# Delta rule with one key product for two matrices, and the write keys shifted through DRAM

## The chip, the cores and the metric

The kernel runs on one core of one Trainium2 chip. All data are 32-bit floats. The metric is the device time of one execution in microseconds (us). A core has TensorE (PE, matrix products and turns of a block against an identity matrix), VectorE (DVE), ScalarE (ACT), GpSimd (POOL) and SyncE (SP), which in this program does nothing but issue DMAs. The five run their own instruction streams, in order, and wait for one another by semaphores.

## The reference, cut to what matters

The program is two layers of a recurrent network: a layer norm, a delta rule, a mixture of experts, a layer norm, a selective scan, a ternary feed-forward net. The change touches the delta rule alone, which has 4 sequences of 1024 rows, 2 heads of 128. `rk` are the read keys (rows of x, each scaled to length 1); the write keys `wk` are the same rows one row later. The reference works in chunks of 64 rows, the kernel in chunks of 128, which gives the same numbers.

```python
rk = rk / jnp.maximum(jnp.linalg.norm(rk, axis=-1, keepdims=True), 1e-12)
wk = jnp.pad(rk[:, :, :-1], ((0, 0), (0, 0), (1, 0), (0, 0)))
...
cum = jnp.cumsum(log_decay, -1)
L_mask = jnp.tril(jnp.exp(jnp.tril(cum[..., :, None] - cum[..., None, :])))
M = jnp.tril(-(wk_scaled @ jnp.swapaxes(wk, -1, -2)) * L_mask, -1)
A = solve_triangular(eye - M, jnp.broadcast_to(eye, M.shape), lower=True, unit_diagonal=True)
intra = jnp.tril(rk @ jnp.swapaxes(wk, -1, -2) * L_mask, -1)
...
def step(S, inp):
    A_i, vsc_i, wkd_i, rkd_i, intra_i, wkp_i, ced_i = inp
    v_new = A_i @ vsc_i - A_i @ wkd_i @ S
    o_i = rkd_i @ S + intra_i @ v_new
    S = ced_i[..., None, None] * S + wkp_i @ v_new
    return (S, o_i)
```

M needs the products of write keys with write keys, scaled by beta (a sigmoid per row) and a decay; intra needs those of read keys with write keys. Since wk is rk one row later, row t of the first matrix is row t-1 of the second up to the factors: the products are the same numbers, shifted by one.

## The kernel before

The time axis is cut into 8 chunks of 128 rows; one step n handles chunk n of all 4 sequences and both heads, so that most instructions are issued twice (h = 0, 1) on tiles of 128 partitions by 4 blocks of 128 (128x512). There are no loops over a scheduler's list: the code of each engine is written out by hand, in functions `sp_a`, `pool_a`, `dve_a`, `act_a` and `pe_a`. The lists `ahead` and `order` (L198, L199) name the steps that fill a PSUM bank in PE's order; from them the program gives out the 4 banks of each head in turn (`gbank`, `gfree`), and the lists of `g_dve`, `g_act` and `g_pool` number what each engine signals. A prime behind a name means chunk n+1, two primes n+2.

I call a turn of the loop `for n in range(NSEQ)` pass n. In pass n PE does: the product `kk` of write keys with write keys of chunk n+1; a turn `d4`; a turn `wkT` of the write keys of chunk n; `wkS`, write keys times state S; the levels 4, 5 and 6 that widen the inverse A from blocks of 16 to 128 rows (P4, D4, P5, t5, D5, t6, P6, T6, with the turn of the next read keys `rkT` before level 6); `MT`, a turn of M of chunk n+1; `vn`; the values `v` of chunk n+1; per head the output `o` and the state product `S`; the product `kq` of read keys with write keys of chunk n+1; and the output projection `y`, whose left operand is OT, ACT's copy of `o`. The keys lie turned in RKT: `prev(n, h)` are columns 0 to 127 (write keys) and `mine(n, h)` columns 1 to 128 (read keys) of 129.

The running sums `cum` of the log decays of a chunk are laid as a row in DRAM (cumd) and loaded into all 128 partitions, as tile ZR (`sums`, L310). From ZR ACT makes three masks: E for M (relu L886, exp L891; with log beta, as bias `nbc`, per partition), ET for intra (relu L900, exp L911, cut to a triangle by POOL as ETsel), and ez (L908) for the read keys times decay, rkdT, which POOL makes. ZR is one tile per head, so the next sums are issued only after ETr and ez of the former.

DVE multiplies bank `kk` by E into M (`mix`, L545) and bank `kq` by ET into iT (`inner`, L561). SP stores the 16x16 blocks of M on the diagonal to DRAM (`blocks`, L317, tile md) and loads them into MB (`spread`, L325), each spread over 16 partitions; POOL inverts them by 31 small steps (`solve`, tiles X and Y); DVE puts X on the diagonal of DT (`inverse`, L551), with which PE begins the levels. In pass n SP issues, in this order: the blocks, the spread, the sums of chunk n+2, the results of pass n-1 (`sd<-XS`), and rows for the expert stage, which POOL scatters by 64 indirect DMAs between its solves (from pass 2 on).

ACT's code for a pass is the following; OT is the last copy before `squares`.

```python
                copy("d4", n, "d4", "Dm")
                if more:
                    copy("wk", n, "wkT", "wk")
...
                if more:
                    upper(n + 1)
                    decays(n + 1, "ET")
...
                copy("vn", n, "vn", "vn")
...
                if n + 2 < NSEQ:
                    lower(n + 2)
                for h in range(2):
                    e.wait_ge(*g_pe[h].at("o", n))
...
                    e.activation(OT[h][:], four(gbank("o", n, h)), ACT.Copy).then_inc(g_act[h].sem, 1)
```

## Time and profile before

| | |
|---|---|
| median of 3 runs | 2403.66 us (2401.52 to 2408.75) |
| the profiled execution's own time | 2399.99 us |
| its span | 2398.3 us |
| busy, share of the span | PE 92%, DVE 77%, ACT 69%, POOL 60% |
| chain that ended last | PE 54%, DVE 13%, issue 9%, ACT 9%, DMA 6%, POOL 6% |
| passes 0 to 7 of the delta rule | about 88 to 404 us of the span |
| mean DMA rate | 179 GB/s |

The span is the part of the execution that the profiler covers; the profiled execution's own time is 1.7 us more. "Busy" is the time in which an engine ran an instruction, summed over all stages of the program, so the shares of the table say little on the delta rule; the views by stretch do. In a timeline, each row is a run of like instructions: its start in the span, how long it lasted, the engine, the line of the kernel, what it writes and reads, how many there were, and in brackets how long the engine had stood idle before it and for what.

### The profile page before, as it was taken

The page shows a single profiled execution, that of the slowest core. Times are in us where ns is not written, and L with a number is a line of the kernel's source. Part 1 is how long each engine was busy: PE and PEld are TensorE (multiplying, and loading weights), DVE is VectorE, ACT ScalarE, POOL GpSimd, SP SyncE. Part 2 cuts the span into 40 slices and gives each one's busy share as a digit, 9 for nine tenths or more (in the row PEclk, how much of TensorE's full clock was granted, in tenths as well). Part 3 has the DMA queues.
Part 4 walks back from the last instruction along what each step waited for, and adds up shares of the span by engine and source line. Part 5 has one row for each costly group of instructions (what it writes and reads, how often), then busy time and mean ns, then how long its engine had stood idle before and what let it go on. Part 6 is the DMA issues. An engine that isn't in the chain of part 4 may idle for free.

```text
span 2398.3 us, 36952 instructions
## 1 busy us (share of the span) xinstructions
PE 2197.5 (92%) x12464; PEld 1788.7 (75%) x12464; DVE 1843.5 (77%) x2832; ACT 1646.8 (69%) x2715; POOL 1449.4 (60%) x1026
## 2 busy tenths in 40 slices
PE   6799897999999999996999999999999999999986
PEld 4788796998898898884667667676676765776765
DVE  5574453667766666677989989989899899898995
ACT  6775542555555556666887788787877877888774
POOL 0236563111111113336988989889889898898895
PEclk8899998999999999997999999999999999999988
DMA  8434544566666654444655655555555555565563
GB/s 291 85 56 111 112 125 136 181 236 232 234 230 230 233 209 152 133 126 154 219 169 190 198 184 186 194 186 202 176 186 195 199 187 177 185 211 177 178 208 101
DMA packets 235434, 430.22 MB, mean 179 GB/s; under 512 B 35089, under 2 KB 117457, under 8 KB 235234
## 3 DMA queue, kind: packets, MB, share of 16 engines
q1 hardware_dynamic: 229090, 410.87, 53.0%
q0 software_dynamic: 6144, 16.79, 2.2%
q8 instruction: 113, 1.85, 0.3%
q14 instruction: 87, 0.71, 0.1%
HBM read 353.61 MB, written 73.96 MB: 178 GB/s over the span
## 4 chain that ended last, share of the span: by engine, by line
PE 54%; DVE 13%; issue 9%; ACT 9%; DMA 6%; POOL 6%; SPq 1%; another core or an unknown queue 1%; POOLq 1%; DVEq 0%; ACTq 0%
PE pb L1641 11%; PE pb L1614 11%; DVE pb L2094 6%; PE pb L2406 5%; PE pb L2411 5%; PE pb L994 3%; PE pb L2305 2%; PE pb L2432 2%; PE pb L2321 2%; DVE UU L2100 2%; DMA XB<-xnd 2%; PE pb L2330 2%; DMA CC<-bcd 2%; POOL UU L2019 2%; POOL UU L2027 1%
## 5 line engine op out<-in xcount | busy, mean ns | idle before, releaser
L2019 POOL TENSOR_TENSOR UU<-dx,BB 128x1024 f32<-128x1024 f32 x256 | 614.6, 2409 | 112.0 <-DMA BB<-bcd 83.6
L2231 ACT ACTIVATE pb<-dt,al 128x512 f32<-128x512 f32 x512 | 339.5, 685 | 149.4 <-DVE UU L2100 147.8
L2100 DVE TENSOR_TENSOR UU<-pb,CC 128x512 f32<-128x512 f32 x512 | 351.3, 686 | 24.3 <-DMA CC<-bcd 6.5
L2094 DVE TENSOR_TENSOR_SCAN pb<-pb,hs,UU 128x512 f32<-128x512 f32 x256 | 328.5, 1283 | 10.7 <-ACT pb L2231 7.4
L2094 DVE TENSOR_TENSOR_SCAN pb<-pb,UU 128x512 f32<-128x512 f32 x256 | 313.0, 1223 | 8.5 <-ACT pb L2231 7.9
L1381 POOL TENSOR_TENSOR clo_b<-craw_b,chi_b 128x1024 fp32r<-128x1024 f32 x22 | 62.3, 2830 | 405.9 <-ACT chi_b L1444 405.9
L1531 DVE TENSOR_TENSOR HL<-HF,HH 128x512 fp32r<-128x512 f32 x220 | 159.6, 728 | 179.9 <-ACT HH L1436 165.7
L2406 PE MATMUL pb<-HAh,WH 128*128 128x512 f32 x1024 | 282.7, 419 | 7.0 <-DVE dt L2075 5.1
L1431 ACT ACTIVATE HF<-pb,BU 128x512 f32<-128x512 f32 x192 | 132.3, 689 | 219.4 <-PE pb L1614 191.9
L2411 PE MATMUL pb<-HAl,WH 128*128 128x512 f32 x1024 | 259.7, 396 | 0.0
L1641 PE MATMUL pb<-W2h,HH 128*128 128x256 f32 x880 | 256.0, 291 | 1.0
L1641 PE MATMUL pb<-W2l,HH 128*128 128x256 f32 x880 | 248.6, 282 | 0.0
L1641 PE MATMUL pb<-W2h,HL 128*128 128x256 f32 x880 | 248.5, 282 | 0.0
L2406 PEld LDWEIGHTS pb<-HAh,WH 128*128 128x128 f32 x1024 | 191.5, 193 | 67.2 <-issue 27.5
L2027 POOL TENSOR_TENSOR UU<-UU,UU 128x1024 f32<-128x1024 f32 x96 | 230.8, 2404 | 5.6 <-DVE UU L2100 5.6
L2411 PEld LDWEIGHTS pb<-HAl,WH 128*128 128x128 f32 x1024 | 195.4, 191 | 44.4
L2305 PEld LDWEIGHTS pb<-ident,UU 128*128 128x128 f32 x1280 | 147.7, 143 | 58.6 <-POOL UU L2027 38.5
L2305 PE MATMUL pb<-ident,UU 128*128 128x128 f32 x1280 | 165.5, 277 | 20.7 <-POOL UU L2027 19.9
L1641 PEld LDWEIGHTS pb<-W2h,HH 128*128 128x128 f32 x880 | 167.5, 190 | 12.0 <-DVE HL L1531 4.8
L1641 PEld LDWEIGHTS pb<-W2h,HL 128*128 128x128 f32 x880 | 167.8, 191 | 5.9 <-issue 1.0
L1641 PEld LDWEIGHTS pb<-W2l,HH 128*128 128x128 f32 x880 | 167.6, 190 | 0.0
L2045 POOL TENSOR_TENSOR HAl<-tg,HAh 128x512 fp32r<-128x512 f32 x128 | 162.9, 1297 | 5.4 <-ACT HAh L2269 5.4
(336 smaller groups left out, 4891.0 us busy)
## 6 DMA issues: line engine op xcount, KB each, us to landing
WH<-fhd SPq DMA_DIRECT2D x176, 512.0 KB, 3.5
BB<-bcd SPq DMA_DIRECT2D x256, 256.0 KB, 4.7
CC<-bcd SPq DMA_DIRECT2D x256, 256.0 KB, 5.0
raw<-in_w1a SPq DMA_DIRECT2D x23, 1024.0 KB, 7.3
raw<-in_w2a SPq DMA_DIRECT2D x23, 1024.0 KB, 7.4
craw_b<-in_fch SPq DMA_DIRECT2D x22, 512.0 KB, 5.9
fhd<-chi_b SPq DMA_DIRECT2D x22, 512.0 KB, 3.9
fld<-clo_b SPq DMA_DIRECT2D x22, 512.0 KB, 4.9
```

Source lines behind the costliest of these rows:

```text
L1531: e.tensor_tensor(HH[q % 4][1][:], HF[q % 2][:], HH[q % 4][0][:].bitcast(F32), ALU.subtract).then_inc(s_hl, 1)
L1614: t = e.matmul(bk[:, a * wide:(a + 1) * wide], wt_[:, k, c_], xt_[k], start=(n == 0), stop=(n == 5))
L1641: t = e.matmul(to[:, j * D:(j + 1) * D], ht[:, c_], wt_[:, row, :], start=(row == 0 and j == 0 and m == 0), stop=(row == 7 and m == 2), sk ...
L2019: e.tensor_tensor(ubuf(n)[:], dx[p][:], BB[n % 3][:].rearrange("p (a m) -> p a m", a=1).to_broadcast([P, 2, 512]), ALU.mult).then_inc(p_u. ...
L2027: e.tensor_tensor(ubuf(n)[:], ubuf(n)[:], ubuf(n - 1)[:], ALU.add).then_inc(p_join.sem, 1)
L2045: e.tensor_tensor(hl[:, it, :], ttile("h", blk, j)[:], hh[:, it, :].bitcast(F32), ALU.subtract).then_inc(f_pool.sem, 1)
L2094: e.tensor_tensor_scan(h_[:], h_[:], uu[:, c, :], first, ALU.mult, ALU.add).then_inc(v_sc.sem, 1)
L2100: e.tensor_tensor(uu[:, c, :], abank(n, c)[:], CC[n % 3][:], ALU.mult).then_inc(v_mu.sem, 1)
L2231: e.activation(abank(n, c)[:], dt[p][:, c, :], ACT.Exp, scale=al1[:, 2 * p + c, s:s + 1]).then_inc(c_a.sem, 1)
L2305: t = e.matmul(ypart(j, c), ubuf(n)[:, c, j * P:(j + 1) * P], ident[:], is_transpose=True, start=False, stop=(s == 15), skip_group_check=True)
L2406: e.matmul(bk[:], WH[n % 3][:, c_], xh_, start=(k == 0), stop=False)
L2411: t = e.matmul(bk[:], WH[n % 3][:, c_], xl_, start=False, stop=(k == 7))
```

## The change

**One product.** `kk` and the turn `MT` stay for chunk 0 alone. For every later chunk the bank of `kq` gives both matrices: its columns 0 to 126 times E make columns 1 to 127 of the turned M, and all of it times ET makes iT. So M is made turned from the start (tiles MTB, two in rotation, in place of M2 and the copies MT), and iT has two tiles (iTB). For this E needs, along the row, cum less log beta, and per partition cum: cumd and ZR become twice as wide (128x4x256 for each head, 512 KB instead of 256 KB as loaded), and the prologue makes the second row by one more product and a tile `nl`. `kq` of chunk n+1 moves from the end of pass n to its start, where `kk` was, and DVE's `inner(n + 1)` from behind S to behind `mix(n + 1)`.

**The write keys.** PE's turn `wkT` and ACT's copies to `wk` go. In their place ACT's `rk` rows are stored to DRAM (`keys_out`, tile rkd, 256 KB for each head) and loaded one row higher (`keys_in`) as `wk`.

**The masks.** ET of chunk n+2 is made in pass n, behind E, in place of ET of chunk n+1 in the middle of pass n. POOL's cut of ET stands behind the solve instead of ahead of it.

```diff
+            def keys_out(n):
+
+                for h in range(2):
+                    e.wait_ge(*g_act[h].at("rk", n))
+                    e.dma_start(rkd[h, :, 1 + n * P:1 + (n + 1) * P, :].rearrange("b t d -> t b d"), TB[h]["rk"][:]).then_inc(s_rkd, 16)
+
+            def keys_in(n):
+
+                e.wait_ge(s_rkd, 32 + 32 * (n + 1))
+                for h in range(2):
+                    if n:
+                        e.wait_ge(*g_pe[h].at("S", n - 1))
+                    e.dma_start(TB[h]["wk"][:], rkd[h, :, n * P:(n + 1) * P, :].rearrange("b t d -> t b d")).then_inc(s_wk, 16)
...
                 if n + 1 < NSEQ:
                     spread(n + 1)
+                if 0 < n < NSEQ - 1:
+                    keys_in(n)
                 if n + 2 < NSEQ:
+                    keys_out(n + 2)
                     sums(n + 2)
...
                     scatter(chunk_pairs(n - 1)[2:])
-                    upper(n + 1)
                     decayed(n + 1)
                     solve(e, n + 1)
+                    if n + 2 < NSEQ:
+                        upper(n + 2)
...
-                e.tensor_tensor(M2[:, h], four(gbank("kk", n, h)), W["E"][:], ALU.mult).then_inc(g_dve[h].sem, 1)
...
+                e.tensor_tensor(MTB[n % 2][:, h, :, 1:P], four(gbank("kq", n, h))[:, :, 0:P - 1], W["E"][:, :, 1:P], ALU.mult).then_inc(g_dve[h].sem, 1)
...
                 if more:
                     for h in range(2):
                         mix(n + 1, h)
+                    for h in range(2):
+                        inner(n + 1, h)
...
                 if more:
                     for h in range(2):
-                        inner(n + 1, h)
-                    for h in range(2):
                         inverse(n + 1, h)
...
                 copy("d4", n, "d4", "Dm")
-                if more:
-                    copy("wk", n, "wkT", "wk")
                 if n + 2 < NSEQ:
                     rows_(n + 2)
-                if more:
-                    upper(n + 1)
-                    decays(n + 1, "ET")
...
                 copy("t6", n, "t6", "DT")
-                if more:
-                    copy("MT", n + 1, "MT", "MT")
                 copy("vn", n, "vn", "vn")
...
                 if n + 2 < NSEQ:
                     lower(n + 2)
+                    upper(n + 2)
+                    decays(n + 2, "ET")
...
                 if more:
-                    for h in range(2):
-                        e.wait_ge(*g_act[h].at("rc", n))
-                        kk(n + 1, h)
+                    inner(n + 1)
                 for h in range(2):
                     e.wait_ge(*g_dve[h].at("DT", n))
                     turned("d4", n, h, TB[h]["DT"])
-                for h in range(2 if more else 0):
-                    turned("wkT", n, h, prev(n, h))
...
-                if more:
-                    for h in range(2):
-                        MT(n + 1, h)
...
-                if more:
-                    inner(n + 1)
                 for b2 in range(2):
                     y(n, b2)
```

What this does to the order of instructions is plainest in three places. A number behind a name tells tiles of the same role apart (E_95 is head 0, E_108 head 1; the change gives the tiles other numbers).

ACT at the end of pass 0, before:

```order
L916 ACTIVATE MT_97<-pb 128x512
L916 ACTIVATE MT_110<-pb 128x512
L916 ACTIVATE vn_102<-pb 128x512
L916 ACTIVATE vn_115<-pb 128x512
L886 ACTIVATE E_95<-ZR_164,sm_nbc 128x128 x4
L886 ACTIVATE E_108<-ZR_165,sm_nbc 128x128 x4
L891 ACTIVATE E_95<-E_95 128x512
L891 ACTIVATE E_108<-E_108 128x512
L974 ACTIVATE OT_125<-pb 128x512
L974 ACTIVATE OT_126<-pb 128x512
```

and with the change:

```order
L952 ACTIVATE vn_101<-pb 128x512
L952 ACTIVATE vn_112<-pb 128x512
L920 ACTIVATE E_96<-ZR_164,sm_cum 128x128 x4
L920 ACTIVATE E_107<-ZR_165,sm_cum 128x128 x4
L927 ACTIVATE E_96<-E_96 128x512
L927 ACTIVATE E_107<-E_107 128x512
L936 ACTIVATE ET_97<-ZR_164,sm_cum 128x128 x4
L936 ACTIVATE ET_108<-ZR_165,sm_cum 128x128 x4
L947 ACTIVATE ET_97<-ET_97 128x512
L947 ACTIVATE ET_108<-ET_108 128x512
L1009 ACTIVATE OT_125<-pb 128x512
L1009 ACTIVATE OT_126<-pb 128x512
```

The copies MT are gone, and the ten instructions of ET stand between E and OT.

SP in pass 1, before:

```order
L317 DMA md<-M_121 128x1x16 x8
L325 DMA MB<-md 16x1920 x8
L310 DMA ZR_164<-cumd 128x4x128
L310 DMA ZR_165<-cumd 128x4x128
L331 DMA sd<-XS 128x256 x4
```

and with the change:

```order
L321 DMA md<-MTB_118 128x1x16 x8
L329 DMA MB<-md 16x1920 x8
L344 DMA wk_94<-rkd 128x4x128
L344 DMA wk_105<-rkd 128x4x128
L336 DMA rkd<-rk_92 128x4x128
L336 DMA rkd<-rk_103 128x4x128
L314 DMA ZR_164<-cumd 128x4x256
L314 DMA ZR_165<-cumd 128x4x256
L349 DMA sd<-XS 128x256 x4
```

Four DMAs of the keys stand ahead of the sums, which are twice as wide.

PE at the start of pass 1 (behind y of pass 0), before:

```order
L994 MATMUL pb<-RKT 128x128 x8
L986 MATMUL pb<-ident,DT_99 128x128 x4
L986 MATMUL pb<-ident,DT_112 128x128 x4
L986 MATMUL pb<-ident,RKT 128x128 x8
L994 MATMUL pb<-S,RKT 128x128 x8
L994 MATMUL pb<-Dm_98,MT_97 128x128 x4
```

and with the change:

```order
L1029 MATMUL pb<-RKT 128x128 x8
L1021 MATMUL pb<-ident,DT_99 128x128 x4
L1021 MATMUL pb<-ident,DT_110 128x128 x4
L1029 MATMUL pb<-S,RKT 128x128 x8
L1029 MATMUL pb<-Dm_98,MTB_118 128x128 x4
```

The first row was kk and is now kq; the turn of the write keys has gone from between d4 and wkS.

## Rows read from the trace of the kernel before

**Rows 1.** Stretches: us; busy PE, PEld, DVE, ACT, POOL; PE clock; DMA share; GB/s.
```profile
122.40:159.90 37.50, 35.80 (x309) 34.31 (x309) 26.92 (x77) 26.39 (x70) 13.93 (x35) 1.00 0.34 57
...
240.90:281.40 40.50, 35.95 (x305) 33.67 (x304) 20.80 (x46) 24.13 (x68) 24.18 (x46) 1.00 0.56 105
```

**Rows 2.** Timelines of ACT and PE, ends of passes 1 and 4.
```profile
148.98 2.45 ACT L886 ACTIVATE E<-ZR,sm_nbc 128x128 f32<-128x128 f32 x8 [2.45 <-DMA ZR<-cumd]
...
156.45 3.62 PE L1033 MATMUL pb<-wr,OT 128*128 128x256 f32 x16
...
273.30 2.44 ACT L886 ACTIVATE E<-ZR,sm_nbc 128x128 f32<-128x128 f32 x8 [7.32 <-DMA ZR<-cumd]
...
277.89 3.69 PE L1033 MATMUL pb<-wr,OT 128*128 128x256 f32 x16 [1.82 <-ACT OT L974]
```

**Rows 3.** View of the tile ZR, 100 to 330 us: idle before it, landing.
```profile
  DMA ZR<-cumd: 28.7, 6
...
DMA to landing us min/median/max: 7.7/9.9/14.3
```

**Rows 4.** Timeline of SP in pass 1 (the time is that of issuing).
```profile
126.61 5.05 SPq L317 DMA_DIRECT2D md<-M  x8
132.93 3.58 SPq L325 DMA_DIRECT2D MB<-md  x8
136.60 0.93 SPq L310 DMA_DIRECT2D ZR<-cumd  x2
```

**Rows 5.** Timeline of PE in pass 1: products and turns, with what follows.
```profile
122.43 1.95 PE L994 MATMUL pb<-RKT 128*128 128x128 f32 x16
124.22 1.04 PE L986 MATMUL pb<-ident,DT 128*128 128x128 f32 x8
125.09 1.04 PE L986 MATMUL pb<-ident,RKT 128*128 128x128 f32 x8
...
143.02 1.09 PE L986 MATMUL pb<-ident,M 128*128 128x128 f32 x8
143.95 1.95 PE L994 MATMUL pb<-vsc,DT 128*128 128x128 f32 x16
...
151.09 1.06 PE L994 MATMUL pb<-vnt,wk 128*128 128x128 f32 x8
```

**Rows 6.** Timeline of ACT, middle of pass 1.
```profile
129.12 2.44 ACT L900 ACTIVATE ET<-ZR,sm_cum 128x128 f32<-128x128 f32 x8
131.58 1.28 ACT L911 ACT_TABLE_LOAD   x1
132.87 1.15 ACT L911 ACTIVATE ET<-ET 128x512 f32<-128x512 f32 x2
```

**Rows 7.** Timeline of DVE, passes 1 and 6.
```profile
155.91 1.44 DVE L561 TENSOR_TENSOR iT<-pb,ET 128x512 f32<-128x512 f32 x2
...
361.66 1.29 DVE L551 TENSOR_TENSOR DT<-X,mask 128x512 f32<-128x512 f32 x2 [0.89 <-POOL X L388]
```

**Rows 8.** POOL behind MB's landing, pass 1; DMA view 221:226 and 24:36; tile TM.
```profile
142.36 0.29 POOL L381 COPY X<-eye 128x128 f32<-128x128 f32 x1 [3.54 <-DMA MB<-md]
...
DMA packets 451, 0.23 MB, mean 46 GB/s; under 512 B 5, under 2 KB 451, under 8 KB 451
...
q1 hardware_dynamic: 451, 0.23, 24.8%
...
DMA packets 3596, 4.73 MB, mean 394 GB/s; under 512 B 143, under 2 KB 3211, under 8 KB 3595
...
DMA to landing us min/median/max: 5.1/5.1/5.1
```

**Rows 9.** Busy time by stretch around a wait of pass 3.
```profile
205.90:210.20 4.30, 0.01 (x1) 0.00 (x0) 0.79 (x3) 4.28 (x15) 1.92 (x2) 0.93 0.38 101
210.30:216.30 6.00, 6.00 (x28) 6.00 (x29) 3.41 (x8) 2.05 (x3) 1.23 (x2) 0.50 0.99 145
```

**Rows 10.** Timeline of DVE in pass 5, behind the scatter.
```profile
294.50 1.12 DVE L717 SCALAR_TENSOR_TENSOR vsc<-pb,sm_bec,vsc 128x128 f32<-128x128 f32 x4 [8.98 <-remote]
```

More of the change, by code:

```diff
@@ L109, in program @@
         sm = {k: sbt("sm_" + k, [P, NT, 2]) for k in ("beta", "nbeta", "g", "cum", "nbc", "ec", "bec", "tl", "tail", "ced")}
+        sm["nl"] = sbt("sm_nl", [P, NT, 2])
         sm.update({k: sbt("sm_" + k, [P, NT, 4]) for k in ("ab", "l")})
         S = sbt("S", [P, 2, B, P])
-        nm = ["rk", "ez", "wk", "vsc", "E", "ET", "MT", "Dm", "DT", "Pm", "iT", "vn", "vnt"]
+        nm = ["rk", "ez", "wk", "vsc", "E", "ET", "Dm", "DT", "Pm", "vn", "vnt"]
         TB = [{k: sbt(f"{k}{h}", [P, 4, P]) for k in nm} for h in range(2)]
         RD = [[sbt(f"rkdT{h}{i}", [P, 4, P]) for i in range(2)] for h in range(2)]
-        M2 = sbt("M2", [P, 2, 4, P])
+        MTB = [sbt(f"MTB{i}", [P, 2, 4, P]) for i in range(2)]
+        iTB = [sbt(f"iTB{i}", [P, 2, 4, P]) for i in range(2)]
         MB = sbt("MB", [P, 15, 8, 16])
@@ L147, in program @@
         rows = [sbt(f"rows{i}", [P, 2, D]) for i in range(3)]
-        cumT = sbt("cumT", [64, P])
-        ZR = [sbt(f"ZR{h}", [P, 4, P]) for h in range(2)]
+        cumT = sbt("cumT", [64, 2, P])
+        ZR = [sbt(f"ZR{h}", [P, 4, 2, P]) for h in range(2)]
         a_end = at[0]
@@ L331, in residuals @@
                     e.dma_start(sd[:, n + 8 * b, :], XS[:, n + 8 * b, :]).then_inc(s_sd, 16)
+            e.dma_start(rkd[:, :, 0, :].rearrange("h b d -> (h b) d"), zt[0:8, 0:P]).then_inc(s_rkd, 16)
+            keys_out(0)
             e.wait_ge(*a_dve.at("cumT"))
-            e.dma_start(cumd, cumT[:]).then_inc(s_zr, 16)
+            e.dma_start(cumd, cumT[:].rearrange("p k t -> p (k t)")).then_inc(s_zr, 16)
             e.wait_ge(s_zr, 16)
@@ L384, in solve @@
                 if k % 2:
-                    e.tensor_tensor(Y16[:, :, r:15], MB[:, r:15, :, r].rearrange("p r g -> p g r"),
+                    col = MB[:, r, :, r + 1:16] if n else MB[:, r:15, :, r].rearrange("p r g -> p g r")
+                    e.tensor_tensor(Y16[:, :, r:15], col,
                                     X16[:, :, r:r + 1].to_broadcast([P, 8, 15 - r]), ALU.mult).then_inc(g_x.sem, 1)
@@ L539, in mix @@
                 W = TB[h]
-                e.wait_ge(*g_pe[h].at("kk", n))
                 e.wait_ge(*g_act[h].at("E", n))
-                if n:
-                    e.wait_ge(*g_pe[h].at("MT", n - 1))
-                    e.wait_ge(s_md, 128 * n)
-                e.tensor_tensor(M2[:, h], four(gbank("kk", n, h)), W["E"][:], ALU.mult).then_inc(g_dve[h].sem, 1)
+                if n == 0:
+                    e.wait_ge(*g_pe[h].at("kk", 0))
+                    e.tensor_tensor(MTB[1][:, h], four(gbank("kk", 0, h)), W["E"][:], ALU.mult).then_inc(g_dve[h].sem, 1)
+                    return
+                e.wait_ge(*g_pe[h].at("kq", n))
+                e.wait_ge(*(g_pe[h].at("MT", 0) if n == 1 else g_pe[h].at("P6", n - 2)))
+                e.wait_ge(s_md, 128 * (n if n == 1 else n - 1))
+                e.tensor_tensor(MTB[n % 2][:, h, :, 1:P], four(gbank("kq", n, h))[:, :, 0:P - 1], W["E"][:, :, 1:P], ALU.mult).then_inc(g_dve[h].sem, 1)
             def inverse(n, h):
@@ L885, in lower @@
                     for b in range(4):
-                        t = e.activation(W["E"][:, b, :], z_[:, b, :], ACT.Relu, bias=sm["nbc"][:, n + 8 * b, h:h + 1])
+                        if n:
+                            t = e.activation(W["E"][:, b, :], ZR[h][:, b, 1, :], ACT.Relu, bias=sm["cum"][:, n + 8 * b, h:h + 1], scale=-1.0)
+                        else:
+                            t = e.activation(W["E"][:, b, :], z_[:, b, :], ACT.Relu, bias=sm["nbc"][:, n + 8 * b, h:h + 1])
                     t.then_inc(g_act[h].sem, 1)
@@ L907, in decays @@
                             e.wait_ge(*g_pool[h].at("rkdT", n - 1))
-                        e.activation(TB[h]["ez"][:], ZR[h][:] if n else four(gbank("z", 0, h)), ACT.Exp).then_inc(g_act[h].sem, 1)
+                        e.activation(TB[h]["ez"][:], ZR[h][:, :, 0, :] if n else four(gbank("z", 0, h)), ACT.Exp).then_inc(g_act[h].sem, 1)
                     else:
@@ L934, in act_a @@
             rows_(1)
-            copy("MT", 0, "MT", "MT")
+            for h in range(2):
+                e.wait_ge(*g_pe[h].at("MT", 0))
+                e.activation(MTB[0][:, h], four(gbank("MT", 0, h)), ACT.Copy).then_inc(g_act[h].sem, 1)
             carried(0)
@@ L1121, in pe_a @@
                         if l == 4:
-                            e.wait_ge(*g_act[h].at("MT", n))
+                            if n:
+                                e.wait_ge(*g_dve[h].at("M", n))
+                            else:
+                                e.wait_ge(*g_act[h].at("MT", 0))
                             e.wait_ge(*g_act[h].at("d4", n))
```

59 lines of the change are left out of this document (35 added, 24 removed).

## The prediction

> **What bounds the kernel now.** I read the busy time by stretch first, then the timelines of PE, ACT and SP inside one pass, then the view of the tile ZR, then the DMA view. The change touches only the delta rule, from about 55 to 404 us of 2398. A pass is one turn of the loop over n; it runs from one kk product to the next (122.4 to 159.9 us is pass 1, 240.9 to 281.4 us pass 4) [rows 1].
>
> The reader is to see two things. First, PE is nearly full: 35.8 us busy in the 37.5 us of pass 1 [rows 1]. That speaks for the change. Second, ACT is not full, but it works to a deadline at the end of each pass. It sits idle until the running sums ZR have landed (2.45 us in pass 1, 7.32 us in pass 4), then makes E, then copies OT, and PE's y product waits for OT [rows 2]. In pass 4 PE already stands 1.82 us for it. All six passes that load sums show this idle time, 28.7 us in all [rows 3]. The sums are issued at 136.60, as the last thing behind md (5.05 us of issue) and MB (3.58 us), and are ready at 148.98: 12.4 us later [rows 2, 4]. So there are two chains of about equal length: PE's own work, and M, md, MB, ZR, E, OT, y. The change shortens the first and lengthens the second.
>
> **The change, part by part.** *Products.* In each pass with a successor PE loses one product of both heads (1.95 us as a row, 1.79 from its start to that of the turn behind it), the turn of wk (1.04; the turn ahead of it takes 0.87 from its start to the next) and the turn of M (1.09, 0.93 up to the next) [rows 5]: 3.6 us, 25 us in seven passes. ACT loses the copies of both, about 1.1 us each. This counts only where PE is last. Worked for pass 1, in us after its start at 122.4: PE would be ready for y at 156.45 - 3.6 - 122.4 = 30.4.
>
> *ET moves.* The relus and exps of ET, 2.44 and 1.15 us [rows 6], leave the middle of the pass, where ACT had time, and stand between E and OT. From E's start to y it takes 4.6 us today when nothing else holds y (273.30 to 277.89) [rows 2]; with ET it takes 4.6 + 3.6 = 8.2. Pass 1 had 7.5 us from E to y (148.98 to 156.45), so it loses 0.7; pass 4 loses 3.6; the other four idled 18.9 us together before E, 4.7 each, between the two, and get 2.0 each. Sum 12. Ahead of the first pass ET also stands before the copy of d4: 3 of its 3.6 us count.
>
> *Sums are issued later.* SP now issues the load of wk and the store of rk ahead of the sums. A pair like it takes 0.93 us [rows 4], so 1.9 us, in pass 0 (store alone) 0.9. The order of SP's queue is the changed program's own. Where the sums wait for the exp ez rather than for SP, two other things stand there: the table load, 1.28 us, which lay ahead of ET's exp [rows 6] and now lies ahead of ez, behind t5; and the two iT products of DVE, 1.44 us [rows 7], which come ahead of Pm instead of after S. Pm feeds D4, D5 and t5, and ez stands behind t5; no row says how much of it DVE's gaps take up, so I take 1.1, between 0 and 1.44. Of 1.9 on the one path and 1.28 + 1.1 = 2.4 on the other I take 2.1 us for each of the six passes: 13. The page "ScalarE: Activation LUTs" of the Trainium skill, section "What ACT_TABLE_LOAD costs", adds a drain of about 1.38 us to each load. Here the exp starts 1.29 us after the load starts [rows 6]; the trace disagrees, and by that rule the sum would be 4 us more over three passes.
>
> *Sums land later.* The store and the load of keys are 1 MB in 2048 pieces of 512 bytes per pass, ahead of the sums; the sums themselves double to 1 MB. No row has these transfers. Bounds for the keys: 0, if they fill gaps; 23 us, if they go as the queue does while sums are under way (451 packets in 5 us, 46 GB/s) [rows 8]. The nearest row is the loading and zeroing at the start, 3596 packets in 12 us, so 6.8 us for 2048 [rows 8]; I take it, because those too read and write distinct addresses. Bounds for the doubling: 0, since the number of pieces stays, or 6.6 us (pass 1: MB landed 142.36, sums ready 148.98) [rows 2, 8]; I take 2.5. In pass 1 the sums are then ready at 142.4 + 6.8 + 6.6 + 2.5 = 158.3 against 148.98 + 1.9 = 150.9: 7.4 more. The same in pass 4; 5 in pass 0, with the store alone; 2 each in passes 2, 3 and 5, where sums are issued some microseconds behind MB and keys drain meanwhile. Sum 26.
>
> *PE's clock.* PE would be ready for y about 31.5 us into a pass and get OT at 37 or later: 6 us or more idle. After 4.3 us idle the granted clock was 0.50, the 1.2 GHz level, through the next 6 us [rows 9], against 1.00 in pass 4, which holds the 1.82 us wait [rows 1]. Half speed for 6 us costs at most 3; part of it lies beside DVE. 2.7 for six passes: 16; bounds 0 and 18.
>
> *At nothing.* wk by DMA: in pass 1 its load would stand first behind MB (landed 142.36) and, at the keys' rate taken above (6.8 us for both), be there after 3.4 us more plus some 2 for landing: 147.8, against its product S at 151.09 less the 1.8 us of the two turns [rows 5, 8]. A margin of 1.5 us is thin; without it S, and with it o and OT, would come later by what is missing, but OT now waits longer for ET anyway. Pass 6 has no E or ET, but its end waits for the solve on POOL (DT, 0.89 us of idle time behind X) [rows 7], so PE's 3.6 us are worth nothing there. The scatter's first eight transfers now wait for ET; they run beside the idle PE. One more product in the prologue, the extra row of cumd and the first rk store: below 1 us.
>
> **Sum.** 12 + 3 + 13 + 26 + 16 = 70. The profiled execution took 2399.99 us; 2400 + 70 = 2470. That execution lies 3.7 us under the median of the runs shown, well inside my range. No change, for this kernel, means within 0.3%, 7 us.
>
> **Rivals.** *A, the sums come early (faster).* If they land as an ordinary load does, ZR's 12.4 us shrink. TM, 512 KB, landed in 5.1 us [rows 8]; two such would be ready about 6.5 us after issue. Pass 1 would last 14.2 (to the issue of the sums) + 2.1 + 6.5 + 8.2 + 3.6 = 34.6 instead of 37.5 us; with half of that where the scatter runs some 10 us are gained: 2390. It decides once the sums are ready less than about 9 us after issue (14.2 + 2.1 + 9 + 8.2 + 3.6 = 37.1). For it: pieces grow from 512 to 1024 bytes. Against it: 7.7 to 14.3 us to landing today [rows 3], and 2048 pieces more ahead of them. [...] *B, within 0.3%:* the sums at 9 to 10 us after issue and no drop of the clock, so that what ET costs and what PE gives back cancel. *C, the sums go by bytes:* 12.4 us become 25; six times 12.4 instead of six times 2.5 is 59 more, 2530. For it: one row is read by 128 partitions, and the rate stayed near 46 GB/s with the DMA engines a quarter busy [rows 8]. *D, the scatter collides:* twelve indirect transfers in a row across the start of a pass, as in pass 5, where DVE stood 8.98 us [rows 10]. It would add about 5 us in three passes: 2485. *E, PE remains the bound:* all 25 us come, 2375; it needs OT at 30.4 us, that is sums ready 6 us after issue; part of A's chance.
>
> **Numbers.** Forecast 0.70, A with E 0.07, B 0.05, C 0.10, D 0.08. Faster 0.07, same 0.05, slower 0.88. Low end: ET, the start and the later issue alone, 12 + 3 + 13 = 28, less 3 if the later issue is partly hidden: 2425. High end: C with some of D, 2540. The likeliest is 2470.
>
> **What will show it.** In the new profile: the idle time of PE ahead of y, with ACT's OT as its releaser, in each of passes 0 to 5, 6 us or more; passes 1 and 2 at 45 to 52 us, pass 1 having had 37.5; ZR still above 10 us to landing; ACT's E, exp, ET, exp, OT in one run behind the landing; a granted clock of about a half ahead of and in y. PE's busy time outside slowed stretches is down 3.6 us a pass. The prediction is wrong if PE's idle time ahead of y is below 2 us, if the sums are ready within 9 us of issue, or if S waits for wk.

## The result, and the profile after

| | before | after |
|---|---|---|
| median of the device time, 5 runs each | 2403.66 us | 2453.61 us |
| lowest and highest | 2400.01, 2414.59 | 2447.82, 2456.65 |
| ratio, with its 95% interval | | 1.0200 (1.0178 to 1.0223) |
| the profiled execution's own time | 2399.99 us | 2456.65 us |
| its span | 2398.3 us | 2454.9 us |

The kernel became 2% slower, 50 us by the medians; 2470 was forecast, with 2425 to 2540 as the range. The two profiled executions lie 57 us apart.

The page of the changed kernel, the shares of busy time and the chain that ended last:

```profile
PE 2189.8 (89%) x12244; PEld 1779.6 (72%) x12244; DVE 1843.3 (75%) x2833; ACT 1631.2 (66%) x2687; POOL 1444.4 (59%) x1026
...
PE 53%; DVE 12%; ACT 10%; issue 10%; DMA 8%; POOL 5%; SPq 1%; POOLq 1%; another core or an unknown queue 0%; DVEq 0%; ACTq 0%
```

PE has less to do and its share fell from 92% to 89%. In the chain DMA went from 6% to 8%. Where the time lies is plain in the two timelines of ACT and PE at the end of pass 1, which answer to [rows 2]:

```profile
165.76 2.44 ACT L920 ACTIVATE E<-ZR,sm_cum 128x128 f32<-128x128 f32 x8 [8.17 <-DMA ZR<-cumd]
168.11 1.13 ACT L927 ACTIVATE E<-E 128x512 f32<-128x512 f32 x2
169.15 2.43 ACT L936 ACTIVATE ET<-ZR,sm_cum 128x128 f32<-128x128 f32 x8
171.48 1.13 ACT L947 ACTIVATE ET<-ET 128x512 f32<-128x512 f32 x2
172.52 1.05 ACT L1009 ACTIVATE OT<-pb 128x512 f32<-128x512 f32 x2
```

```profile
164.83 1.06 PE L1029 MATMUL pb<-vnt,wk 128*128 128x128 f32 x8
173.72 5.88 PE L1068 MATMUL pb<-wr,OT 128*128 128x256 f32 x16 [7.83 <-ACT OT L1009]
179.43 1.95 PE L1029 MATMUL pb<-RKT 128*128 128x128 f32 x16
```

The reader is to see one unbroken run on ACT behind the landing of the sums (E, exp, ET, exp, OT) and beside it PE, done at 165.9 and idle for 7.83 us. Then y takes 5.88 us, where it took 3.62. The busy time by stretch shows the whole of pass 1, the idle time, and y (columns as in [rows 1]):

```profile
134.50:179.40 44.90, 34.69 (x277) 32.43 (x276) 26.25 (x74) 23.13 (x64) 13.47 (x35) 0.89 0.45 83
...
165.90:173.70 7.80, 0.00 (x0) 0.01 (x1) 2.32 (x6) 7.80 (x24) 1.23 (x2) 0.63 0.05 16
173.70:179.50 5.80, 5.78 (x17) 4.75 (x18) 1.01 (x4) 4.47 (x18) 0.00 (x0) 0.62 0.00 0
```

SP in pass 1 answers to [rows 4]:

```profile
137.30 5.05 SPq L321 DMA_DIRECT2D md<-MTB  x8
143.62 4.35 SPq L329 DMA_DIRECT2D MB<-md  x8
148.07 0.93 SPq L344 DMA_DIRECT2D wk<-rkd  x2
149.04 1.06 SPq L336 DMA_DIRECT2D rkd<-rk  x2
150.20 3.87 SPq L314 DMA_DIRECT2D ZR<-cumd  x2
```

From issue to E's start it is now 15.6 us (150.20 to 165.76), against 12.4. In the code E waits for the sums of both heads, and SP needs 3.87 us to issue the two DMAs instead of 0.93: the second is issued at 153.3 us and lands 12.4 us later, just ahead of E. The view of the tile ZR, 90 to 400 us, gives the idle time of ACT ahead of E and the landing, answering to [rows 3]:

```profile
  DMA ZR<-cumd: 55.0, 6
...
DMA to landing us min/median/max: 7.9/12.5/14.0
```

**Where the 57 us lie.** A pass of 0 to 5 can be cut into four pieces that follow one another without a gap: from its start to the issue of the sums, from there to E, from E to y, and y. The pieces are read from the timelines of each profiled kernel; a pass starts where y of the pass before ends, the first piece of pass 0 counts from the span's start, and each sum is over passes 0 to 5, in us.

| kernel | to issue | issue to E | E to y | y | passes 6 and 7 | y of pass 7 ends |
|---|---|---|---|---|---|---|
| before | 194.2 | 77.3 | 33.4 | 21.9 | 77.6 | 404.4 |
| after | 204.3 | 90.8 | 47.8 | 35.5 | 80.6 | 458.9 |
| difference | 10.1 | 13.4 | 14.4 | 13.6 | 3.0 | 54.5 |

Another 2 us came about behind the delta rule. The column of passes 6 and 7 is made of pass 6, 40.7 us against 36.7, and pass 7, 39.9 against 40.9.

The piece from issue to E holds two things, the time in which SP issues the two DMAs and the landing of the second. SP's part is 16.1 us in the six passes, against 5.6 before; without it 74.6 us are left, against 71.7. So of the 13.4 us only 2.9 are later landing, and 10.5 are slower issuing.

### The profile page after: what moved, and what is told of

The parts are those of the page before. It is cut to its first block, busy times and chain, and to the rows that moved or that the text cites. A ratio compares the mean times of both kernels' runs of the same rounds, so it can differ in the third digit from the quotient of the medians.

```text
span 2454.9 us, 36493 instructions
## 1 busy us (share of the span) xinstructions
PE 2189.8 (89%) x12244; PEld 1779.6 (72%) x12244; DVE 1843.3 (75%) x2833; ACT 1631.2 (66%) x2687; POOL 1444.4 (59%) x1026
## 4 chain that ended last, share of the span: by engine, by line
PE 53%; DVE 12%; ACT 10%; issue 10%; DMA 8%; POOL 5%; SPq 1%; POOLq 1%; another core or an unknown queue 0%; DVEq 0%; ACTq 0%
PE pb L1672 11%; PE pb L1645 11%; DVE pb L2125 6%; PE pb L2437 5%; PE pb L2442 5%; DMA ZR<-cumd 4%; PE pb L2336 2%; PE pb L2352 2%; PE pb L1029 2%; PE pb L2463 2%; PE pb L2405 2%; PE pb L2361 2%; DMA XB<-xnd 2%; DVE UU L2131 2%; DMA CC<-bcd 2%
```

## The experiments

Every kernel below is the changed kernel with one edit, unless it says otherwise. The ratio is to the kernel before on the same chip. The chips differ: the kernel before took 2403.03 us beside the four kernels from et_behind_ot to warm, 2412.11 beside keys_around and the three from early_head to early_tail, 2401.30 beside scatter_first and early_scatter, and 2407.33 beside early_split and before_ez. So ratios are the safer comparison across these groups.

| kernel | median, us | ratio to before (95% interval) |
|---|---|---|
| the change | 2453.61 | 1.0200 (1.0178 to 1.0223) |
| et_behind_ot | 2448.55 | 1.0180 (1.0151 to 1.0210) |
| no_keys | 2428.00 | 1.0112 (1.0081 to 1.0144) |
| sums_single | 2445.85 | 1.0170 (1.0142 to 1.0199) |
| warm | 2448.79 | 1.0189 (1.0162 to 1.0216) |
| keys_around | 2429.69 | 1.0078 (1.0053 to 1.0104) |
| scatter_first | 2433.50 | 1.0136 (1.0119 to 1.0153) |
| early_head | 2428.81 | 1.0072 (1.0049 to 1.0096) |
| early_wk | 2424.96 | 1.0058 (1.0031 to 1.0085) |
| early_tail | 2417.46 | 1.0030 (1.0012 to 1.0047) |
| early_scatter | 2396.31 | 0.9985 (0.9968 to 1.0001) |
| early_split | 2393.21 | 0.9935 (0.9914 to 0.9956) |
| before_ez (edit of the kernel before) | 2409.18 | 1.0007 (0.9989 to 1.0024) |

And the pieces of those that change one thing, as in the table above:

| kernel | to issue | issue to E | E to y | y | passes 6 and 7 | y of pass 7 ends |
|---|---|---|---|---|---|---|
| et_behind_ot | 228.1 | 82.6 | 27.5 | 31.0 | 83.7 | 452.9 |
| no_keys | 192.5 | 75.7 | 47.8 | 35.2 | 80.7 | 431.9 |
| sums_single | 202.1 | 83.9 | 47.8 | 35.5 | 80.2 | 449.4 |
| warm | 206.1 | 89.2 | 53.5 | 27.6 | 77.5 | 454.0 |
| keys_around | 191.7 | 77.0 | 47.8 | 33.2 | 80.8 | 430.4 |
| scatter_first | 191.7 | 89.7 | 47.8 | 35.8 | 74.2 | 439.1 |

### The keys ahead of the sums: no_keys, keys_around

```diff
-                if 0 < n < NSEQ - 1:
-                    keys_in(n)
                 if n + 2 < NSEQ:
-                    keys_out(n + 2)
                     sums(n + 2)
```

(The waits for these DMAs go with them.)

> The changed kernel without the stores and loads of the keys in the passes: wk keeps the rows of chunk 0 for all chunks, so the state product is made from the wrong rows; times only. Theory as forecast: the 1 MB of keys ahead of the sums costs both issue time (1.9 us a pass) and landing time. From the issue of the sums to E it takes 15.1 us on the mean of six passes in the changed kernel and 12.9 in the kernel before; without keys it should be back near 13, and the issue comes 1 to 2 us earlier: 12 + 8 = 20 us less, 2434. Rival (the keys fill gaps, the landing is longer because the sums have doubled): issue to E stays at 15, and only the issue comes earlier, 2446.

Measured: 2428. Issue to E fell from 90.8 to 75.7 us, 12.6 a pass, so the rival falls: sums of twice the width land as fast as the single ones did in the kernel before (77.3) once no keys are ahead of them. Of the 15.1 us, 10.5 are SP's time for issuing the sums (16.1 us in six passes with the change, 5.6 here), and 4.5 are landing. The issue came 12 us earlier in all, more than the 8 expected.

keys_around keeps every byte and moves only the place in SP's queue:

```diff
+                if 0 < n < NSEQ - 1:
+                    keys_in(n)
                 if n + 1 < NSEQ:
                     blocks(n + 1)
...
-                if 0 < n < NSEQ - 1:
-                    keys_in(n)
                 if n + 2 < NSEQ:
-                    keys_out(n + 2)
                     sums(n + 2)
+                    keys_out(n + 2)
```

> The changed kernel with SP's order in a pass turned: the load of wk ahead of the blocks of M (SP waits there for M anyway), the sums right behind the spread, the store of rk behind the sums. All transfers stay. Without keys the kernel took 2428, with them 2454: 26 us. If it is the order (keys issued and queued ahead of the sums), most of that comes back: issue of the sums to E near 12.6 us, 2432. Rival (it is the bytes in the queue, wherever they stand; the store now runs beside the landing sums): issue to E stays at 15 and only the 1.9 us of issue come back, 2446.

Measured: 2429.69, ratio 1.0078, and issue to E 77.0 us. Its SP, ACT and PE in pass 1:

```profile
145.12 0.93 SPq L314 DMA_DIRECT2D ZR<-cumd  x2
146.10 3.58 SPq L336 DMA_DIRECT2D rkd<-rk  x2
149.73 3.85 SPq L349 DMA_DIRECT2D sd<-XS  x4
160.04 3.00 SPq L344 DMA_DIRECT2D wk<-rkd  x2
```

```profile
157.06 2.44 ACT L920 ACTIVATE E<-ZR,sm_cum 128x128 f32<-128x128 f32 x8 [2.72 <-DMA ZR<-cumd]
```

```profile
165.03 3.69 PE L1068 MATMUL pb<-wr,OT 128*128 128x256 f32 x16 [2.39 <-ACT OT L1009]
```

E starts 11.9 us behind the issue although the store of keys is issued right behind the sums; the load of the next wk stands at the end of the pass, where the queue is empty. Pass 1 takes 37.3 us, and 37.5 in the kernel before. SP issues the sums in 0.93 us in five of the six passes. So it was the order and not the bytes: of the 2.0% that the change costs, 1.2 points went with the places in SP's queue (0.9 with no_keys, whose interval overlaps this one). Whether the load or the store did more was not tried apart.

### The doubled sums: sums_single

```diff
-                    e.dma_start(ZR[h][:].rearrange("p b k t -> p b (k t)"), cumd.rearrange("(b n h) t -> n h b t", b=4, n=8)[n, h].rearrange("(o b) t -> o b t", o=1).to_broadcast([P, 4, 2 * P])).then_inc(s_zr, 16)
+                    e.dma_start(ZR[h][:, :, 0, :], cumd.rearrange("(b n h) t -> n h b t", b=4, n=8)[n, h, :, 0:P].rearrange("(o b) t -> o b t", o=1).to_broadcast([P, 4, P])).then_inc(s_zr, 16)
...
-                            t = e.activation(W["E"][:, b, :], ZR[h][:, b, 1, :], ACT.Relu, bias=sm["cum"][:, n + 8 * b, h:h + 1], scale=-1.0)
+                            t = e.activation(W["E"][:, b, :], ZR[h][:, b, 0, :], ACT.Relu, bias=sm["cum"][:, n + 8 * b, h:h + 1], scale=-1.0)
```

> The changed kernel with the sums loaded in single width (512 bytes a piece, 256 KB a head), E being made from the row that ET uses; the factor beta is left out of M, times only. If the doubling is worth 2.5 us a pass, as forecast, from the issue of the sums to E takes 12.6 instead of 15.1 us and the time falls by 15 us to 2439. If pieces count and bytes do not, both stay: 2454. If bytes set the landing (rival C) it would fall by 6 us or more a pass, 2418.

Measured: 2445.85. Issue to E is 83.9 us, 14.0 a pass: 1.2 less than with double width, between the first two answers. Of these 6.9 us in six passes 3.0 are again SP's issuing (13.2 us against 16.1). By the times alone the intervals of this kernel and of the change overlap (1.0142 to 1.0199, 1.0178 to 1.0223). With no_keys beside it, the doubling costs at most about 1 us a pass behind the keys, and nothing that shows without them. Rival C, landing by bytes, falls.

### ET behind OT: et_behind_ot

```diff
                     lower(n + 2)
-                    upper(n + 2)
-                    decays(n + 2, "ET")
                 for h in range(2):
                     e.wait_ge(*g_pe[h].at("o", n))
...
+                if n + 2 < NSEQ:
+                    upper(n + 2)
+                    decays(n + 2, "ET")
```

> The changed kernel with ET's relus and exps of chunk n+2 moved behind the copy to OT; nothing else. Theory (the chain ZR, E, ET, OT, y sets the length of passes 0 to 5): from E's start to y it takes 4.6 us instead of 7.96 in each of six passes, PE's idle time ahead of y falls from 7.8 to about 4.5 us in passes 1 to 3, and the time falls by about 20 us, to 2434. Rival (another wait ends at the same time as OT, so ET is covered): PE's idle time ahead of y keeps its length under another releaser, and the time stays at 2454. Second rival: ET now delays the copy of d4 at the start of the next pass and half is given back, 2444.

Measured: 2448.55. E to y fell to 4.59 us in every pass, 20.2 us in all, as the theory has it. But the piece up to the issue grew by 23.7 us. The second rival is right in kind, by another road than the copy of d4 alone, and more is given back than the half that it had (2448.55 against 2444). ACT and DVE at the start of pass 1:

```profile
123.09 2.44 ACT L936 ACTIVATE ET<-ZR,sm_cum 128x128 f32<-128x128 f32 x8
125.42 1.14 ACT L947 ACTIVATE ET<-ET 128x512 f32<-128x512 f32 x2
129.91 1.28 ACT L965 ACT_TABLE_LOAD   x1
131.21 0.21 ACT L965 ACTIVATE rn<-rn 128x8 f32<-128x8 f32 x1
131.32 1.06 ACT L952 ACTIVATE Dm<-pb 128x512 f32<-128x512 f32 x2
```

```profile
131.45 0.17 DVE L603 TENSOR_SCALAR rn<-rn 128x8 f32<-128x8 f32 x1 [6.64 <-ACT rn L965]
```

The squares and the square root of the key norms stand behind OT on ACT, and now behind ET too. The first instruction of a pass on DVE waits for that root, and M, the blocks and the sums stand behind it on DVE and SP. A deadline that the change had not touched lay 4 to 5 us behind OT.

### PE kept busy ahead of y: warm

```diff
                 e.wait_ge(*gfree("y", n, b2))
+                for j in range(36 if b2 == 0 and n < NSEQ - 2 else 0):
+                    e.matmul(bk[:, 0:P], ident[:], ident[:], start=True, stop=True)
```

> The changed kernel with 36 products of the identity matrix into y's own bank ahead of y in passes 0 to 5 (y overwrites them), so that PE is busy for about 8 us of the wait for OT. Theory (y is slow, 5.9 instead of 3.6 us, because PE stood idle ahead of it): y takes 3.6 us again in passes 1 to 3, less surely in passes 4 and 5, where 5 us of idle time are left; the time falls by 9 to 14 us, to 2440 to 2445. Rival (the granted clock follows something else, such as the load of the whole chip): y stays at 5.9 us and the time at 2454.

Measured: 2448.79, where 2440 to 2445 were expected. The busy time by stretch of this kernel, the wait and y of pass 1:

```profile
165.50:172.00 6.50, 6.50 (x61) 6.50 (x60) 0.94 (x2) 6.47 (x20) 1.22 (x2) 1.00 0.01 1
172.00:175.60 3.60, 3.60 (x20) 3.19 (x19) 0.00 (x0) 3.39 (x14) 0.00 (x0) 1.00 0.00 0
```

With PE busy through the wait the granted clock is 1.00 and y takes 3.62 us in passes 0 to 3; in passes 4 and 5, where 4.5 and 5.8 us of idle time are left, it takes 6.6 and 6.5. So the slow y comes from the idle time, and the rival falls. The products themselves held y up in passes 0 to 3 by 0.4 to 3.5 us (E to y 53.5 against 47.8), so of the 7.9 us won in y little is left, and by time this kernel is not told apart from the change.

### The scatter's place: scatter_first

The changed kernel cuts ET on POOL behind the solve and ahead of the scatter of two pairs of rows. This edit swaps the two:

```diff
                     solve(e, n + 1)
-                    if n + 2 < NSEQ:
-                        upper(n + 2)
                 else:
                     scatter(chunk_pairs(n - 1)[2:])
                 scatter(chunk_pairs(n)[:2])
+                if n + 2 < NSEQ:
+                    upper(n + 2)
```

> The changed kernel with the same move alone: POOL's scatter right behind the solve, the cut of ET behind it. In passes 3 to 5 the scatter's stalls lie beside the wait for OT, so little is to be had there; pass 6, 40.7 us against 36.7 before, has no such wait and should be back at 37, and ez and with it the sums come some us earlier in passes 3 to 5 (they stand behind t5 at 18 to 24 us into the pass). 4 us from pass 6 and up to 2 us in each of three passes: 2446. Rival (pass 6 is longer for another reason, such as iT ahead of the levels): 2454.

Measured: 2433.5, 20 us less than the change by the medians and 15 by the ratios, where 8 were expected. In the changed kernel the start of pass 6 (378.35 us) looked as follows on POOL (the fifth and the last of a row of twelve), DVE and PE:

```profile
378.23 0.96 POOL L475 DMA_INDIRECT xg<-rows,sl  x1 [0.31 <-issue]
...
387.10 0.96 POOL L475 DMA_INDIRECT xg<-rows,sl  x1 [0.30 <-issue]
```

```profile
390.40 1.13 DVE L749 SCALAR_TENSOR_TENSOR vsc<-pb,sm_bec,vsc 128x128 f32<-128x128 f32 x4 [6.93 <-remote]
```

```profile
385.79 1.53 PE L1029 MATMUL pb<-Dm,MTB 128*128 128x128 f32 x8 [3.00 <-issue]
391.00 2.04 PE L1029 MATMUL pb<-Dm,MTB 128*128 128x128 f32 x8 [3.68 <-issue]
```

POOL had waited 8.27 us for ET, so the eight indirect DMAs of the end of pass 5 began only at 373.06 us and ran on into the four of pass 6, and PE and DVE stood 6.7 and 6.9 us beside the end of the row and up to 3 us behind it, for nothing that the profile names. With the scatter ahead, the eight and the four are parted (the eighth starts at 362.29 us, the ninth at 367.79). Pass 6 of this kernel, and behind it that of the kernel before, are

```profile
364.90:398.10 33.20, 30.79 (x267) 29.29 (x266) 18.75 (x41) 7.09 (x14) 17.12 (x38) 1.00 0.69 171
```

```profile
326.60:363.30 36.70, 34.44 (x297) 32.80 (x296) 19.55 (x44) 12.50 (x28) 21.88 (x43) 1.00 0.60 155
```

It is 33.2 us long, 7.5 less than with the change and 3.5 less than before: here, in a pass without sums, PE's saving is seen in full. But the larger part of the gain is in the passes with sums. Passes 3 to 5 are 4.0, 5.2 and 1.8 us shorter, 11.0 together, where up to 6 were expected; their sums were issued 7.3, 1.5 and 2.2 us earlier. So the cost of the scatter's place was not hidden beside the wait for OT: with the sums later, OT came later too. (Another 2.6 us are in pass 0, where nothing is scattered yet; this edit does not explain them.)

### Taking the sums off the path: early_wk, early_tail, early_head

These three make ET and ez of chunk n+2 behind OT of pass n, so that ZR is free at the end of the pass, and move the squares and the root to the middle of the next pass, behind the rk rows (which takes away what undid et_behind_ot).

```diff
                 if n + 2 < NSEQ:
                     rows_(n + 2)
+                if n + 3 < NSEQ:
+                    for b in range(4):
+                        squares((n + 3 + 8 * b,))
+                    roots(n + 3)
...
                 if more:
-                    decays(n + 1, "ez")
                     carried(n + 1)
...
                     lower(n + 2)
-                    upper(n + 2)
-                    decays(n + 2, "ET")
...
+                if n + 2 < NSEQ:
+                    upper(n + 2)
+                    decays(n + 2, "ET")
+                    decays(n + 2, "ez")
```

early_wk takes the write keys as the kernel before does (turn and copy). early_tail keeps them in DRAM, in the order of keys_around. early_head is early_tail with `sums(n + 2)` as the first thing in SP's pass.

> The changed kernel with the write keys turned by PE and copied by ACT as in the kernel before (no keys through DRAM), ET and ez of chunk n+2 made behind OT in pass n, so that ZR is free at once and SP issues the next sums right behind the spread, about 14 us into each pass, and the squares and square roots in the middle of the pass. If the chain through ZR is what costs, E is made about 27 us into the pass, PE's idle time ahead of y is below 1 us, passes 1 and 2 take 36 us or less and the sum of the delta rule comes under the kernel before: 2392. Rival: passes 2 to 5 are held by the scatter on POOL and the stalls beside it, so they stay near 44 us and the time is 2410.

> As early_wk, but with the keys through DRAM in the order of keys_around. PE has 0.9 us and ACT 1.1 us less to do in a pass; the sums land later by what the keys cost there. If the order of SP has healed the keys, 2390; if their bytes still delay the sums by 2.5 us, E comes about 30 us into a pass and y waits 2 us: 2405.

> As early_tail, but the sums of chunk n+2 are issued as the first thing of pass n, ahead of the blocks of M. The chain through ZR is then some 14 us shorter and E never waits; passes 1 and 2 should be PE's own 34 us, 2378 in all. Rival: 1 MB of sums and 512 KB of keys now run beside md and MB, MB lands later than 20 us into the pass and DT waits for the solve: passes stay at 37 us or more, 2400.

Measured: 2424.96, 2417.46 and 2428.81. Pass 1 does what was expected of the first two (36.1 and 35.1 us), pass 2 does not quite (38.5 and 38.3 us, where 36 or less were expected of early_wk). In all three y waits for OT in none of passes 0 to 6, and y takes 3.69 us in passes 0 to 5. The keys through DRAM are worth 1 us in pass 1; by time early_wk and early_tail are not told apart. But passes 3 to 6 of early_tail take 45.7, 46.6, 45.6 and 54.5 us, and what stands there is again the scatter, on POOL at the end of pass 4 and on DVE in it:

```profile
291.88 1.22 POOL L455 TENSOR_SCALAR_AFFINE_SELECT ET<-ET 128x512 f32<-128x512 f32 x2 [14.29 <-ACT ET L947]
```

```profile
264.13 1.29 DVE L758 TENSOR_TENSOR Pm<-pb,mask 128x512 f32<-128x512 f32 x2 [11.07 <-remote]
```

ET comes later still, so twelve indirect DMAs run in a row across the start of each of passes 3 to 6 (246.64 to 261.6 us at the start of pass 4), and DVE stands 11.07 us. The misses of early_wk and early_tail have this cause, as early_scatter below confirms; the rival of early_wk named it, though with 2410 it too fell short. Pass 6 is not all loss: a second row of twelve runs within it, which in the other kernels falls into pass 7, and pass 7 takes 26.5 us instead of some 40. In early_head E never waited for ZR, as expected, but its own rival is right as well, in one pass: in pass 0, the blocks' way to MB is now shared with 1 MB of sums. POOL waits 20.57 us for MB (11.20 in early_tail), and DT for the solve; pass 1 takes 44.5 us, against 35.1 in early_tail:

```profile
118.68 0.29 POOL L407 COPY X<-eye 128x128 f32<-128x128 f32 x1 [20.57 <-DMA MB<-md]
```

```profile
130.74 2.13 DVE L584 TENSOR_TENSOR DT<-X,mask 128x512 f32<-128x512 f32 x2 [7.12 <-POOL X L415]
```

### Both together: early_scatter, early_split

early_scatter is early_tail with the swap of scatter_first. early_split also puts POOL's rkdT between the two groups of indirect DMAs:

```diff
+                    decayed(n + 1)
                     if chunk_pairs(n - 1):
                         e.wait_ge(*g_dve[1].at("M", n + 1))
                     scatter(chunk_pairs(n - 1)[2:])
-                    decayed(n + 1)
                     solve(e, n + 1)
```

> As early_tail, with POOL's scatter of two pairs of rows right behind its solve, as in the kernel before, and its cut of ET (upper) behind that. In early_tail POOL waits 14 us with the scatter behind it for ET, then issues 12 indirect DMAs in a row across the start of the pass, and DVE stands 11.07 us until they end; passes 3 to 5 take 46 us and pass 6 takes 54. Theory (the scatter's place is what is left): the stall falls to that of four DMAs in a row, passes 3 to 5 take 38 to 42 us and pass 6 below 42; the time falls from 2417 by 15 to 30 us, to 2395, under the kernel before beside it (2412 on that chip, 2403 on others) by 0.3% to 1%. Rival (eight DMAs cost the same wherever they stand, since all engines stall beside them): passes 3 to 5 stay near 45 us, 2415.

> As early_scatter, with POOL's rkdT ahead of the four indirect DMAs at the start of a pass instead of behind them, so that the eight at the end of a pass and the four are parted by 3.5 us (cut of ET and rkdT) instead of 1.2. If a long row of indirect DMAs is what holds PE, ACT and DVE, passes 3 to 5 (40.4, 43.4, 40.4 us) lose 1 to 3 us each: 2391, and faster than the kernel before by about 0.4%. Rival (only their number counts, or MB now lands while POOL still scatters): no change, 2396.

Measured: 2396.31, ratio 0.9985 (0.9968 to 1.0001), and 2393.21, ratio 0.9935 (0.9914 to 0.9956). The lengths of passes 1 to 6, in us:

| kernel | 1 | 2 | 3 | 4 | 5 | 6 |
|---|---|---|---|---|---|---|
| before | 37.5 | 37.5 | 43.5 | 40.5 | 45.2 | 36.7 |
| after | 44.9 | 47.9 | 51.0 | 50.7 | 49.1 | 40.7 |
| early_tail | 35.1 | 38.3 | 45.7 | 46.6 | 45.6 | 54.5 |
| early_scatter | 35.1 | 37.2 | 40.4 | 43.4 | 40.4 | 39.0 |
| early_split | 35.1 | 38.3 | 40.2 | 40.8 | 37.3 | 38.0 |

early_scatter came out at the 2395 us expected, but its interval does not part it from the kernel before, and pass 4 is longer than the 38 to 42 us expected. early_split is faster than both kernels, by 0.65% against the one before. Its interval and early_scatter's do not overlap, but the medians lie only 3.1 us apart, and the rest of that difference is the kernel before, which was 6 us slower on early_split's chip. Passes 4 and 5 are 2.6 and 3.1 us shorter, but pass 3 only 0.1, and pass 2 is 1.0 longer. In early_scatter twelve DMAs ran in a row at the start of pass 4 and of pass 6 and are parted in early_split, which fits; at the start of pass 5 they were parted already (278.72 and 286.60 us), so splitting does not explain that pass. The effect of the split is not shown. Pass 1 of early_split, beside that of before in [rows 1]:

```profile
126.80:161.90 35.10, 32.56 (x278) 30.83 (x278) 26.12 (x74) 23.09 (x66) 13.37 (x36) 1.00 0.53 106
```

PE is busy 32.6 us instead of 35.8, and the pass is 2.4 us shorter. This is what the one product and the shifted keys gave in a pass once nothing else held it. How much of the 0.65% is theirs is open: early_split also has ET, ez, the squares and rkdT in other places, and the kernel before with all these moves was not run.

### The kernel before with ez earlier: before_ez

```diff
                     upper(n + 1)
                     decays(n + 1, "ET")
+                    decays(n + 1, "ez")
...
-                    decays(n + 1, "ez")
                     carried(n + 1)
```

> The kernel before with ez of chunk n+1 made right behind ET of chunk n+1 instead of behind t5, so that the sums need not wait for level 5. In the kernel before the sums are issued 14, 15, 22, 17 and 23 us into passes 1 to 5; with the change they follow the spread, 13 to 16 us where the scatter lets them. Theory (PE's own work bounds most of its passes, the chain through ZR is hidden but for 2 us): 2 to 4 us less, 2400 beside 2403. Rival (ez ahead of t5 delays t5 by 1.1 us and with it level 5 in seven passes): 5 us more.

Measured: no difference, 1.0007 (0.9989 to 1.0024). The sums were issued 5.2 and 3.5 us earlier in passes 3 and 5, and pass 3 is 2.8 us shorter, but passes 1, 2 and 6 are 0.7, 1.2 and 1.8 us longer, and in the profile the delta rule ends 3.6 us later. Both answers fit in part and nearly cancel. So earlier sums alone, got in this way, do not make the kernel before faster. That early_split needs PE's shorter work for its gain fits this but is not shown by it, since only ez was moved here.

## Why the prediction was right

It named the wait, its releaser and the order of its size. PE ahead of y stands 7.8, 7.6 and 7.2 us in passes 1 to 3 ("6 us or more" was forecast), passes 1 and 2 take 44.9 and 47.9 us (45 to 52, so the first is just under), the sums are 12.5 us to landing at the median ("above 10"), E, exp, ET, exp and OT run without a gap, and the clock ahead of and in y is 0.63 and 0.62. Only pass 0, with 4.79 us of idle time ahead of y, fell short of 6. PE's busy time in pass 1, less the 2.2 us by which y is slow there, is 32.5 us against 35.8, 3.3 less where 3.6 were forecast. The mechanism was right; that the total came within 20 us is in part luck, since the largest term was twice too high and another, put at nothing, was not nothing. By its terms:

- **Products.** 3.6 us a pass, covered while y waits for OT: right. That they are worth nothing in pass 6 "since its end waits for the solve" was wrong, as scatter_first shows: 33.2 us against 36.7. The 0.89 us of idle time of DVE there was a thin reason.
- **ET moves**, 12 forecast: E to y rose by 14.4 us. The step gave four passes 2.0 us each; three of them rose by 2.3 to 2.5, and pass 0, which had no slack (4.59 us from E to y), by 3.4. It is right in kind. What the prediction did not see is that moving ET behind OT gives back only 6 us of the profiled end.
- **The start and the later issue**, 3 + 13 forecast: 10.1 together. Pass 0 has 5.1 of it, as forecast, and the issue came 1.5, 4.8, 1.8 and 1.8 us later in passes 1 to 4. In pass 5 it came 4.9 us earlier: the kernel before had the scatter's row of twelve across the start of that pass, ahead of ez [rows 10], and the changed kernel has it across the start of pass 6.
- **Landing**, 26 forecast: 13.4. This is the term that was mis-sized, and most of the excess of the sum. Of the 26, 15 were the doubling and 11 the keys. The doubling is worth nothing without keys ahead of it (75.7 us from issue to E in no_keys, 77.3 before) and 6.9 us with them (sums_single). The keys' size was near: 15.1 us in six passes, 4.1 and 4.7 in passes 1 and 4, for which 4.9 each were forecast. But their way was another: 10.5 of the 15.1 us are SP's issue of the sums behind them, 16.1 us instead of 5.6, while the prediction kept the 0.93 us of [rows 4] for each pair; only 4.5 are landing.
- **PE's clock**, 16 forecast: 13.6 in y. That idle time slows y is shown by warm. The 37 us at which OT was to come, and with it "6 us or more", do not follow from the prediction's own terms: they put E of pass 1 at 35.9 us and y at 44.1, with PE ready at 30.4 or 31.5, so 12 to 14 us of idle time. 7.8 came, since the sums were earlier than that.
- **At nothing.** wk never arrived late: the view of its tile lists no idle time for it. That the scatter's DMAs "run beside the idle PE" was wrong. This is rival D, which had the mechanism and nearly the size (15 us): with the scatter's place alone put back, passes 3 to 5 are 11.0 us shorter and pass 6 7.5. D expected a row of twelve in three passes with sums; it came across the starts of passes 3 and 6, the latter without sums, where it cost 4.0 us against the kernel before.

Rivals A, B and E needed the sums within 9, 10 and 6 us of their issue; the least that came was 12.7 in pass 0. Rival C falls with no_keys.

Against the table of pieces the terms were off by 2 to 13 us, two of them too small (ET, and passes 6 and 7, put at nothing) and three too large; together they gave 70 against 54.5 us in the profiles. The pieces are places in time and not causes: the scatter's 15 to 20 us and the 26 us of the keys' order lie across several of them, and they overlap, so they do not add.

## What to carry to other kernels

A change that takes work from the busiest engine and gives it to a chain that already ends at the same time makes the kernel slower by the chain, not faster by the engine; find the chain's deadline (here OT) and ask what now stands ahead of it, on each queue that it passes. The place of a transfer in a queue can matter more than its bytes: 1 MB a pass more ahead of the sums cost some 26 us, and the same megabyte around them next to nothing; a good part of that cost was the time in which SP issued the sums, not their landing. When one step is moved off the path, look for the next deadline on the same engine, and for what is queued behind a wait on the others, as the scatter was behind POOL's wait for ET.

## What the runs showed of the hardware

- Where twelve indirect DMAs ran in a row on POOL (1.27 us each from start to start), other engines stood idle: DVE 6.9 us and PE 3.0 and 3.7 us in the changed kernel, DVE 11.07 us in early_tail, with no releaser in the profile but "remote" and "issue". With their place alone changed (scatter_first) the delta rule ends at 439.1 instead of 458.9 us. What holds the engines is not shown.
- Loads that spread one row over 128 partitions landed as fast with pieces of 1024 bytes as with 512: 12.6 us a pass from issue to use without keys (no_keys), against 12.9 in the kernel before. Behind the keys the wider sums took up to 1.2 us a pass more (sums_single).
- The idle time just ahead of y does not alone decide its clock. y took 3.69 us after 2.31 us of idle time (et_behind_ot, pass 4) and after 2.39 (keys_around, pass 1), but 5.38 after 1.99 (no_keys, pass 1). What else counts was not followed up.
- SP needed 3.9, 4.4 and 4.4 us to issue the two DMAs of the sums in passes 1, 4 and 5 of the changed kernel, where they follow a run of others (20 in pass 1) without a pause. In passes 0, 2 and 3, where SP had stood 0.7, 5.0 and 6.3 us ahead of them, it needed 0.96, 0.91 and 1.5 us, and in the kernel before, behind 16 others, 0.93. Why was not tried.
